# Score parts of a graph attention stored by head, loaded in rows of 512 bytes, and added after a transpose of the source scores alone

## What is computed (cut to what matters)

```python
ft = (feat @ W_fc).reshape(N, H, D)            # H = 8 heads of 32
eh = jnp.einsum('nhd,hd->nh', ft, attn_h)      # source score of a node
et = jnp.einsum('nhd,hd->nh', ft, attn_t)      # target score of a node
ee = jnp.einsum('ehd,hd->eh', fe, attn_e)      # score of an edge
e = jax.nn.leaky_relu(eh[src] + ee + et[dst], negative_slope=NEG_SLOPE)
e_max = jax.ops.segment_max(e, dst, num_segments=N)
ex = jnp.exp(e - e_max[dst])
a = ex / jax.ops.segment_sum(ex, dst, num_segments=N)[dst]
rst = jax.ops.segment_sum(ft[src] * a[:, :, None], dst, num_segments=N) + bias
```

## Time and profile before

| | |
|---|---|
| median of 3 runs | 3993.47 us (3991.43 to 3995.88) |
| the profiled execution | 4013.74 us, span 4012.0 us |
| TensorE, VectorE, ScalarE, GpSimd busy | 61%, 50%, 32%, 45% of the span |
| mean granted TensorE clock | 0.703 of full speed |
| the attention stage | from 521.9 us to about 1741 us of the span |
| packets of the queue that SyncE feeds | 175446, of them 100352 of the score loads (49 loads of 2048 rows of 32 bytes) |

### The profile page before, as it was taken

How to read it: one execution, slowest core, us unless ns; L and a number is a source line. 1 busy time by engine, 2 the same in 40 slices (tenths; PEclk the granted TensorE clock), 3 DMA queues, 4 the chain that set the end, 5 groups by cost and what they waited for, 6 DMA issues and landing times. The chain is left out here.

```text
span 4012.0 us, 51163 instructions
## 1 busy us (share of the span) xinstructions
PE 2464.4 (61%) x12916; PEld 2133.0 (53%) x12916; DVE 2006.2 (50%) x6412; ACT 1289.1 (32%) x4654; POOL 1800.5 (45%) x1888
## 2 busy tenths in 40 slices
PE   6950956666666666657899834554554554646358
PEld 5850845555555555645676634444444444535347
DVE  7930257777777777756745522222232232364325
ACT  2310223334333334442323322332332332362113
POOL 0046055666666666303000166666666666231255
PEclk9975656666666667668989866666666666855569
DMA  6343333333333333344000133333333333420033
GB/s 189 98 100 92 110 96 89 90 90 89 90 89 90 91 91 90 87 146 123 14 21 21 38 92 92 89 92 92 89 92 92 89 92 93 117 71 1 27 125 95
DMA packets 263656, 348.46 MB, mean 87 GB/s; under 512 B 153545, under 2 KB 193599, under 8 KB 262119
## 3 DMA queue, kind: packets, MB, share of 16 engines
q0 software_dynamic: 87936, 235.05, 20.9%
q1 hardware_dynamic: 175446, 110.32, 10.7%
HBM read 288.25 MB, written 61.20 MB: 87 GB/s over the span
## 5 line engine op out<-in xcount | busy, mean ns | idle before, releaser
L1383 POOL DMA_INDIRECT Gb<-normed_rows,SRCT x784 | 743.2, 948 | 742.5 <-SPq L1375 352.4
L1404 PE MATMUL pAb<-HOTb,Gb 128*128 128x128 f32 x3136 | 574.4, 336 | 578.1 <-issue 563.7
L1404 PEld LDWEIGHTS pAb<-HOTb,Gb 128*128 128x128 f32 x3136 | 521.7, 247 | 631.2 <-issue 614.3
L1444 DVE TENSOR_TENSOR ACC<-ACC,pAb 128x256 f32 x784 | 330.9, 422 | 807.8 <-DMA sums_by_rank<-rrowa 619.3
L975 POOL DMA_INDIRECT GX<-ft_rows,SRCT x432 | 412.0, 954 | 262.9 <-PE apA L1130 127.5
L1057 ACT ACTIVATE ACC<-apA 128x254 f32 x784 | 300.9, 384 | 701.9 <-PE apA L1130 303.1
L1130 PE MATMUL apA<-AHOT,GX 128*128 128x129 f32 x1920 | 396.0, 391 | 171.1 <-DVE GX L1285 146.7
L1130 PEld LDWEIGHTS apA<-AHOT,GX 128*128 128x128 f32 x1920 | 373.0, 298 | 197.0 <-DVE GX L1285 167.2
L1423 ACT ACTIVATE HOTb<-OFFb 128x1024 f32<-128x1024 f32 x98 | 103.6, 1057 | 776.4 <-DMA sums_by_rank<-rrowa 751.4
L975 POOL DMA_INDIRECT G<-ft_rows,SRCT x288 | 274.5, 953 | 172.9 <-PE apA L1130 88.2
L1130 PE MATMUL apA<-AHOT,G 128*128 128x129 f32 x1216 | 244.7, 384 | 101.0 <-DVE G L1285 85.5
(11 more groups left out here) (386 smaller groups left out, 4627.1 us busy)
## 6 DMA issues: line engine op xcount, KB each, us to landing
ebuf<-in_edge_attr_dram SPq DMA_DIRECT2D x49, 448.0 KB
Gb<-normed_rows,SRCT POOLq DMA_INDIRECT x784
rows_by_expert<-ffn_PADT SPq DMA_DIRECT2D x1, 10360.0 KB
sT<-rows_by_expert SPq DMA_DIRECT2D x80, 129.5 KB
GX<-ft_rows,SRCT POOLq DMA_INDIRECT x480
sums_by_rank<-rrowa SPq DMA_DIRECT2D x49, 128.0 KB, 1.7
sums_by_rank<-rrowb SPq DMA_DIRECT2D x49, 128.0 KB, 1.7
GX<-in_x_dram SPq DMA_DIRECT2D x11, 560.0 KB
```

The costliest lines, as they stand in the source:

```text
L1383: pool.indirect_dma_start(G[g % R][m][:, :], None, TABLE[:, :], bass.IndirectOffsetOnAxis(ap=SRCT[:, t:t + 1], axis=0)).then_inc(g_in[g % ...
L1404: last = nc.tensor.matmul(pA[b][:, o:o + EP], G[k][m][:, c * 128:(c + 1) * 128], HOT[k % 2][:, m, :], start=True, stop=True)
L1444: last = nc.vector.tensor_tensor(acc[:, :, ds(b, EP)], acc[:, :, ds(b, EP)], pA[q][:, o:o + KD * EP].rearrange("p (c r) -> p c r", c=KD), ...
```

## The change

`score_parts` is stored by head: its shape becomes 8 x 100352. ScalarE writes `V` by head (the same 128 numbers a row, 16 at a time), VectorE adds `F` in that order (it reads `F` with a step of 8), and each of the seven stores writes runs of 112 numbers (448 bytes) where it wrote runs of 896 (3584 bytes). In `attend` a load brings 128 rows of 512 bytes, already with one head of one tile on each partition. The source scores alone are copied by ScalarE into a new tile `EH`, transposed by TensorE, and VectorE adds `PRE` to the transposed scores, applies the leaky ReLU there and scans the result in SBUF. The order changes with it: on TensorE the transpose stands behind the products of the first two tiles, on VectorE the first two weightings stand together ahead of the scores and the maxima, and ScalarE takes the exponential two tiles later.

```diff
-    PRED = dram("score_parts", (EA, H0))
+    PRED = dram("score_parts", (H0, EA))
...
+        VH = V[:, :].rearrange("p (h j) -> p h j", h=H0)
...
-                    sp.dma_start(pv[:, a], V[:, a]).then_inc(parts_out, 16)
+                    sp.dma_start(pv[:, :, a], VH[:, :, a]).then_inc(parts_out, 16)
...
-                    nc.vector.tensor_tensor(V[:, a], V[:, a], F[:, a], ALU.add).then_inc(parts_ready, 1)
+                    nc.vector.tensor_tensor(VH[:, :, a], VH[:, :, a],
+                                            F[:, :].rearrange("p (j h) -> p h j", h=H0)[:, :, a], ALU.add).then_inc(parts_ready, 1)
...
-                pv = PRED.rearrange("(t p) h -> p t h", p=EP)
+                pv = PRED.rearrange("h (t q) -> h t q", q=EP)
...
-                    sp.dma_start(PRE[k][:, :, :], pv[:, ds(c * UT, UT), :]).then_inc(pre_in[k], 16)
+                    sp.dma_start(PRE[k][:, :], pv[:, ds(c * UT, UT), :]).then_inc(pre_in[k], 16)
...
+                def source_scores(c):
+
+                    act.wait_ge(g_in[c % GS], 16 * UT * (c // GS + 1))
+                    if c:
+                        act.wait_ge(u_ready, c)
+                    nc.scalar.activation(EH[:, :].rearrange("p (h m) -> p m h", h=H0), G[c % GS][:, :, D:RW],
+                                         ACT.Copy).then_inc(e_ready, 1)
...
-                    steps = {3: exponentials, 9: chain}
+                    steps = {0: source_scores, 5: exponentials, 9: chain}
...
                     pe.wait_ge(e_ready, c + 1)
-                    nc.tensor.transpose(pU[:, 0:EP], SC[:, :, :].rearrange("p h m -> p (h m)"),
-                                        ident[0:EP, 0:EP]).then_inc(u_ready, 1)
+                    if c:
+                        pe.wait_ge(pre_free, SL + c)
+                    nc.tensor.transpose(pU[:, 0:EP], EH[:, :], ident[0:EP, 0:EP]).then_inc(u_ready, 1)
...
-                    steps = {0: scores, 8: ends}
+                    steps = {2: scores, 8: ends}
...
-                    dve.wait_ge(g_in[c % GS], 16 * UT * (c // GS + 1))
+                    dve.wait_ge(u_ready, c + 1)
                     dve.wait_ge(pre_in[k], i * 16 + 16)
-                    nc.vector.tensor_tensor(SC[:, :, :].rearrange("p h m -> p m h"), G[c % GS][:, :, D:RW], PRE[k][:, :, :], ALU.add)
-                    dve.drain()
-                    dve.sem_inc(pre_free, 1)
-                    nc.vector.scalar_tensor_tensor(SC[:, :, :], SC[:, :, :], SLOPE, SC[:, :, :], ALU.mult,
-                                                   ALU.max).then_inc(e_ready, 1)
+                    nc.vector.tensor_tensor(SC[:, :], pU[:, 0:EP], PRE[k][:, :], ALU.add).then_inc(pre_free, 1)
+                    dve.drain()
+                    nc.vector.scalar_tensor_tensor(SC[:, :], SC[:, :], SLOPE, SC[:, :], ALU.mult, ALU.max)
+                    dve.drain()
...
+                    weight(c, k, 0)
+                    weight(c, k, 1)
                     if more:
                         scores(n, kn, rn)
-                    weight(c, k, 0)
-                    if more:
                         maxima(n)
-                    weight(c, k, 1)
-                    if more:
                         onehots(n, kn, 0)
```

More of the change, by code:

```diff
@@ L484, in _ @@
                     load(c)
[L485 removed]
+                pv = PRED.rearrange("h (p j) -> p h j", j=ES)
                 for h in range(NPT):
[L487 removed]
+                    a = slice(h * HF, (h + 1) * HF)
                     sp.wait_ge(parts_ready, h + 1)
[L489 removed]
+                    sp.dma_start(pv[:, :, a], VH[:, :, a]).then_inc(parts_out, 16)
                 sp.wait_ge(parts_out, 16 * NPT)
@@ L630, in keep @@
                         act.wait_ge(zero_in, 32)
-                    nc.scalar.activation(V[:, c * C * H0:(c + 1) * C * H0], pS[:, 0:C * H0], ACT.Copy).then_inc(v_ready, 1)
+                    nc.scalar.activation(VH[:, :, c * C:(c + 1) * C], pS[:, 0:C * H0].rearrange("p (j h) -> p h j", h=H0),
+                                         ACT.Copy).then_inc(v_ready, 1)
                 def root(q):
@@ L866, in attend @@
         HOT = [sb(s, f"AHOT{k}", [EP, UT, HW]) for k in range(2)]
-        PRE = [sb(s, f"PRE{k}", [EP, UT, H0]) for k in range(SL)]
+        PRE = [sb(s, f"PRE{k}", [128, EP]) for k in range(SL)]
         LOWC = sb(s, "LOWC", [128, 1])
-        SC = sb(s, "SCT", [EP, H0, UT])
+        SC = sb(s, "SCT", [128, EP])
+        EH = sb(s, "EHT", [EP, 128])
         CT = sb(s, "CTU", [128, EP + 1])
         PEN = sb(s, "PENU", [128, EP + 1])
-        U = {n: sb(s, f"U_{n}", [128, EP]) for n in ("f", "b", "m", "ex", "fs", "bs", "a", "first", "own", "rest")}
+        U = {n: sb(s, f"U_{n}", [128, EP]) for n in ("f", "b", "m", "ex", "fs", "bs", "a", "first", "own")}
+        U["rest"] = U["f"]
         WPEN = sb(s, "WPEN", [128, NCH])
@@ L1184, in maxima @@
                 def maxima(c):
-                    dve.wait_ge(u_ready, c + 1)
                     dve.wait_ge(pen_ready, c + 1)
-                    nc.vector.tensor_tensor_scan(U["f"][:, :], PEN[:, 0:EP], pU[:, 0:EP], LOW, ALU.add, ALU.max)
-                    nc.vector.tensor_tensor_scan(U["b"][:, ::-1], PEN[:, 1:EP + 1][:, ::-1], pU[:, 0:EP][:, ::-1], LOW,
+                    nc.vector.tensor_tensor_scan(U["f"][:, :], PEN[:, 0:EP], SC[:, :], LOW, ALU.add, ALU.max)
+                    nc.vector.tensor_tensor_scan(U["b"][:, ::-1], PEN[:, 1:EP + 1][:, ::-1], SC[:, ::-1], LOW,
                                                  ALU.add, ALU.max)
```

7 lines of the change are left out of this document (3 added, 4 removed).

## The result

The changed kernel takes 4001.25 us (median of 9 runs, 3994.04 to 4006.18) where the kernel before takes 3991.43 in the same comparison (9 runs, 3987.91 to 3995.88): ratio 1.0029, 95% interval 1.0016 to 1.0043. It is about 10 us slower; 4.7 us faster was forecast. A second comparison gave 1.0032 (1.0017 to 1.0047).

The account below looks back on a forecast made before the run. It took a closed loop of four links, 24.91 us a pass, to bound the attention stage while gathers run. -9.5 + 4 + 0.8 = -4.7 took the median from 3993.5 to 3989 us, own range 3980 to 4001.

Parts of the forecast that it names:

- The rule of late signals: Attention stage: in a long run of gathers TensorE's late signals come when it has landed, about 2.75 us after last gather's start.
- the loop's links: Pass: scan to third weighting 9.54, to third gather group 3.81, to last gather 8.81, to next scan 2.75; 24.91 us.
- Sum -1.11 + 0.74 + 0.15 = -0.22 us a pass: Loop: second weighting leaves (-1.11), add and ReLU enter (+0.74), transpose signals later (+0.15); bounds -0.37 and 0.00 us.
- 43 x -0.22 = -9.5: Attention stage: the loop's gain over some 43 passes (3 to 45), in which the late signals hold, 9.5 us faster.
- the other three links: Loop from third weighting through tiles 9 to 12, third and fourth gather groups, to next scan; no gain claimed there.
- the prediction's last rival: Attention loop: the change takes no effect, 0.00 a pass, end's +4.8, 3998 us; inside the forecast's range, no own chance.
- I take 0: Front stage: VectorE's strided read of F and ScalarE's strided write of V keep their element counts, so cost 0.
- +0.8 for the store: End of front: last store writes 1024 runs of 448 bytes for 128 of 3584; +0.8 us, between -0.4 and +2.3.
- The last passes, +4: Three passes behind the last gather: transpose waits for two tiles' products, +1.3 us each, +4 us, upper bound 5.4.
- Short packets: Rival, PRE loads: their short packets hold TensorE's signals, so the wait would vanish; -142 us, 3851 us, chance 0.08.
- The joint maxima's late signal: Rival, attention stage: first two gather groups form one run, delaying L1089's signal ahead of joint maxima; +35, 4033 us, chance 0.17.
- The cheaper operations: Rival, loop: signal there at once, three operations reading SBUF save 8 to 11 ns each; -12.4, 3981 us, chance 0.05.

Follow-up runs that it names:

- A: Chip of follow-up runs on which the kernel before takes 3991 us; TensorE's signals come late there, and the main result also fits it.
- B: Chip of follow-up runs on which the kernel before takes 4016 to 4022 us; TensorE's signals come late there.
- C: Two chips that behave alike, on which the kernel before takes 3495 and 3491 us; TensorE's signals are prompt, within 0.04 us.
- The clean pair: Whole changed kernel against the kernel before, both profiled on one chip: ratio 1.0042 (1.0027 to 1.0057), mean passes 25.28 against 25.12 us (25.20 in another profile).

## Why the prediction was wrong

**The rule of late signals, the loop's links.** Right on A and B: in the median pass the scan or add follows the last gather's start by 2.66 to 2.94 us in the old and the new order, and each edit by itself changed its link by what was written (+0.76 for +0.74, -1.11 for -1.11). But it belongs to the chip, not to the program: on C the same program has no such wait. The prediction read it as the stage's.

**"Sum -1.11 + 0.74 + 0.15 = -0.22 us a pass", 43 x -0.22 = -9.5: this step failed.** It changes the loop by -0.37 ahead of the third weighting and +0.15 at the signal, and holds "the other three links" at what one pass showed. The clean pair on B gives, by the means of the table: -0.28 or -0.29 for the first link, where -0.37 was written; +0.02 to +0.12 for the products of tiles 9 to 12, which should "wait for the third weighting as before"; +0.04 or +0.05 for the two groups of gathers; and +0.29 or +0.30 from the last gather to the signal, where +0.15 was written. The sum is +0.08 to +0.16 in place of -0.22. So no single term fails: the last link gives the largest part, about 0.15 of the 0.30 to 0.38. The links taken as fixed were not.

A part of this is in ordinary passes, those with two separate runs of gathers. There the last link is 2.93 for 2.80 and 2.67, and the products take 4.07 for 3.88 and 3.84, more of them at a lower clock, as the rows below show. (Their median over all passes does not show this by itself: it is 3.90 to 4.14 in the five profiles with the old attention stage.) The rest is that 16 passes in place of 12 and 5 are of the longer kind with one run.

TensorE's row behind the third weighting, before, in the pass of the earlier trace rows, and its granted clock (last but two) in two parts of it:

```profile
1019.83 5.27 PE L1130 MATMUL apA<-AHOT,G 128*128 128x129 f32 x32 [2.13 <-DVE G L1285]
```

```profile
1019.83:1023.30 3.47, 3.47 (x18) 3.47 (x19) 3.01 (x14) 1.34 (x6) 1.85 (x2) 0.57 0.43 119
1023.30:1025.10 1.80, 1.79 (x17) 1.60 (x15) 1.44 (x11) 1.33 (x7) 1.22 (x2) 1.00 0.00 0
```

And after, for the row of 6.16 us above:

```profile
1023.80:1027.60 3.80, 3.80 (x17) 3.80 (x18) 3.27 (x16) 1.51 (x7) 1.74 (x2) 0.50 0.40 107
1027.60:1029.90 2.30, 2.30 (x18) 2.18 (x16) 1.93 (x17) 1.35 (x7) 1.71 (x2) 0.77 0.17 35
```

After the change the four tiles that GpSimd waits for run wholly at the lower level (0.50, 1.2 GHz) and take 3.8 us; before, the clock had risen within the fourth, and they took 3.5. The products stay at the lower level through this link in 28 of 43 passes of the changed kernel on B in 14 and 15 of the kernel before there, and in 20 and 16 with the changed front alone. What TensorE must have done before for the clock to rise was not tested. Shown on one chip: +0.08 to +0.16 a pass, +3 to +7 us instead of -9.5. For A there is no profile of before. Taking the front (5 us), the start and the tail from the measured differences of three kernels there (+10, +33, -14 us) and dividing by 43 puts its pass at 24.8 to 24.9, so the change at 0.0 to +0.1. That is argued, not shown, and which link takes the gain back on A stays open. It is what the prediction's last rival says, no effect in the loop: its 3998 us is the forecast nearest to the result.

**"I take 0" for the strided read of `F`, and +0.8 for the store.** The add takes 1.77 for 1.09 us, on the path once, and with the store 1.3 in place of 0.8. The front's ratio on B says 4 to 6 us in all; on C it is within the uncertainty of none. Why copies of `V` come later was not found.

**The last passes, +4.** Three passes take 63.5 to 64.8 us where they took 59.1 to 59.7, but the pass that follows is further along when they end: from the scan of pass 45 to the end of the stage it is 97.0 to 98.4 for 94.6 to 95.2, on the mean +3.0 (the two profiles of the changed front on B, with the old order, have 96.0 and 96.6). What was left out is the same shift at the start: from the stage's start to the third scan 61.7 to 61.8 for 59.0 to 60.4, on the mean +1.9. Together 5 us at most, near the 4.

**The sum** with measured terms: on B 3 to 7 + 4 to 6 + 5 = 12 to 18 us, against 13.5 between the medians (17 by the ratio). On A 0 to 6 + 1.3 to 5 + 5 = 6 to 16, against 10. Every part has the sign of a loss, and the prediction had one large gain.

**The rivals.** Short packets: refuted on C, and on B by the stage's unchanged length. The joint maxima's late signal: VectorE has no idle time ahead of that copy in any profile of before or after. But the long run of gathers that this rival starts from did come, in 16 of 43 passes on B, 7 on A and 3 in the result's profile, and in most of them VectorE stood behind the copy, in the joint maxima. Part of the rival's loss is there on B, in another place than it said. In the other passes GpSimd's wait ahead of its second group did not go, it shrank from 1.68 to 1.49 in the pass shown, and that ahead of the third grew from 1.60 to 2.03. The cheaper operations: the Trainium skill, "VectorE: DVE Perf Modes", section on the TRN2 errata, has 120 fixed cycles with a PSUM source and 58 with one in SBUF; an estimate from it is 62 cycles saved on each operation whose source moved. The trace does not agree: the same scan has 421 ns from `pU` and 424 from `SCT`, the same subtraction 292 and 292.

## What to carry to other kernels

Where a gain rests on a closed loop, take each link as the mean of all its passes, since only means add up, and look at the unusual passes by themselves. Ask which links contain another engine's work: a gain of 0.2 us a pass is less than what products at a lower clock, a slightly later signal, or a few more passes of the longer kind take. Don't subtract single profiles; take a second one of the unchanged kernel, and compare stages that the change cannot touch: they also tell whether two profiles are from one chip. And a wait that hides a bad order may belong to the chip: put a transpose ahead of the work that doesn't need it, since where signals are prompt its place is paid in full.

## What the hardware showed that was not expected

- The same program takes 3491 and 3495 us on two chips and 3991 to 4022 on two others. Gathers are issued at the same pitch (1.25 to 1.26 us) on all; on one of the first two the pass takes 20.05 us, on B 25.1 to 25.2, with VectorE waiting 4 us a pass for TensorE's transpose, which ended 3 us earlier. What differs between the chips is open.
- On A and B signals late in a run of gathers come, in the median pass, 2.66 to 2.94 us after the start of its last gather. In such a run of eight the attention (`apV`, transposed during the fourth gather, VectorE waiting 0.42 us) was prompt, and the scores, transposed during the seventh, were not.
- A VectorE add of 128x896 takes 1.77 us in place of 1.09 when one operand is read at a step of 8 numbers and the other, with the result, by head in runs of 112. The two were not tried apart.
- The attention stage alone (old front, contiguous rows) cost 1.0070 on B, more than the whole change, 1.0042; its pass was 25.56 us for 25.28. The intervals overlap. All of its 43 passes are of the kind with one run of gathers, for 16 of the whole change there; why is open.
- On A and B VectorE stands, named by no engine, among small dependent operations only while the first two groups of gathers run as one, and hardly ever in the kernel before (2 of 27 such passes against 61 of 69 with the new data flow and order).
